# A four-layer transformer kernel: tokens quantised ahead of the weights, bias vectors split side by side in partitions, and six key tiles computed inside the first attention core

## The reference

```python
# layer 0: int8 fake quantisation of normalised tokens and of two weights
s = maximum(max(abs(x), axis=-1) / 127, 1e-8); qdq(x) = clip(round(x / s), -127, 127) * s
q = qdq(layernorm(x)) @ qdq(wq).T + bq
k, v = split(cond @ wkv.T + bkv)
o = softmax(q k^T / 4) v            # 16 heads of 16 features, per sequence
x = x + tanh(g) * (qdq(o) @ qdq(wp).T + bp)
# layer 1, attention: keys of the same context
k1 = cond @ Wkv[:, :256] + bkv[:256]
```

## Time and profile before

| what | value |
|---|---|
| median of 3 runs | 811.41 us (810.72 to 813.89) |
| the profiled execution, its own time | 810.61 us |
| span of the profiled execution, first to last instruction | 808.6 us |
| mean granted clock of PE | 0.978 |
| busy share of the span | PE 88%, DVE 68%, ACT 48%, POOL 45% |
| opening, until the first score matmul of the core | 46.15 us |

### The profile page before, as it was taken

How to read it: one execution, slowest core, us unless ns; L and a number is a source line. 1 busy time by engine, 2 the same in 40 slices (tenths; PEclk the granted TensorE clock), 3 DMA queues, 4 the chain that set the end, 5 groups by cost and what they waited for, 6 DMA issues and landing times.

```text
span 808.6 us, 13964 instructions
## 1 busy us (share of the span) xinstructions
PE 712.4 (88%) x4726; PEld 400.6 (50%) x4726; DVE 552.4 (68%) x1213; ACT 390.0 (48%) x704; POOL 365.1 (45%) x407
## 2 busy tenths in 40 slices
PE   7989899999998877777878898898989999999883
PEld 4644457434553222223335454455469967677431
DVE  5979966467569899999997977865621135126764
ACT  4367724211027998889993554563203343331211
POOL 3523113164413678788885804002240046992335
PEclk9999998899999899999999999999999999999997
DMA  9700003006307899999997004503841141992012
GB/s 309 127 1 1 1 2 98 1 1 131 78 0 143 152 183 196 176 183 193 186 183 110 1 1 122 155 2 114 184 171 61 47 150 59 266 274 59 1 20 33
DMA packets 226764, 84.41 MB, mean 104 GB/s; under 512 B 188755, under 2 KB 224752, under 8 KB 226704
## 3 DMA queue, kind: packets, MB, share of 16 engines
q1 hardware_dynamic: 223760, 78.38, 45.1%
q0 software_dynamic: 2944, 5.25, 2.7%
HBM read 33.26 MB, written 8.40 MB: 52 GB/s over the span
## 4 chain that ended last, share of the span: by engine, by line
PE 48%; DVE 17%; DMA 15%; POOL 10%; issue 6%; ACT 3%; POOLq 0%; DVEq 0%; SPq 0%; ACTq 0%
DMA hT<-hT 8%; POOL hT L1415 5%; PE psum L925 5%; DMA xn<-hT 4%; PE psum L1939 4%; PE psum L896 4%; PE psum L1605 3%; DVE cx L2567 2%; DVE am L808 2%; PE psum L484 2%; POOL moe_in L2070 2%; PE psum L2218 2%; PE psum L638 2%; DVE arena L1732 2%; PE psum L1947 2%
## 5 line engine op out<-in xcount | busy, mean ns | idle before, releaser
L1480 DVE TENSOR_SCALAR_CACHE_REDUCE psum<-psum,arena 128x1024 f32<-128x1024 f32 x128 | 158.6, 1286 | 10.3 <-PE psum L1302 9.5
L355 POOL TENSOR_TENSOR rstd<-ve,neg_half 128x1 f32<-128x1 f32 x64 | 39.6, 623 | 167.3 <-DVE ve L345 166.8
L1302 PE MATMUL psum<-arena 128*128 128x512 bf16 x256 | 79.0, 391 | 37.8 <-ACT arena L1386 24.9
L1415 POOL TENSOR_SCALAR hT<-arena 128x1024 f16<-128x1024 f32 x86 | 89.8, 1044 | 41.6 <-ACT arena L1386 22.2
L1386 ACT ACTIVATE arena<-psum,am 128x1024 f32<-128x1024 f32 x86 | 95.8, 1115 | 15.2 <-POOL hT L1415 9.6
L1302 PEld LDWEIGHTS psum<-arena 128*128 (+1 forms) x256 | 15.2, 97 | 73.3 <-issue 32.9
L1415 POOL TENSOR_SCALAR hT<-sg 128x1024 f16<-128x1024 f32 x42 | 43.9, 1045 | 12.0 <-DMA hT<-hT 4.4
L1386 ACT ACTIVATE sg<-psum,am 128x1024 f32<-128x1024 f32 x42 | 46.8, 1115 | 4.1 <-POOL hT L1415 2.2
L1290 PE MATMUL psum<-hT,arena 128*32 128x256 f16 x352 | 42.6, 282 | 2.2 <-DMA hT<-hT 2.2
L2077 POOL DMA_INDIRECT arena<-moe_out,route x16 | 16.0, 998 | 59.9 <-DMA moe_out<-arena 55.9
L1853 ACT ACTIVATE arena<-psum 128x1024 f32<-128x1024 f32 x32 | 31.0, 1021 | 22.3 <-PE psum L1810 22.3
(11 more groups left out here) (441 smaller groups left out, 1654.0 us busy)
## 6 DMA issues: line engine op xcount, KB each, us to landing
hT<-in_L_ffn_expert_masks SPq DMA_DIRECT2D x32, 256.0 KB, 3.8
arena<-in_L_ffn_w_gate SPq DMA_DIRECT2D x2, 1408.0 KB
arena<-in_L_ffn_w_up SPq DMA_DIRECT2D x2, 1408.0 KB
arena<-in_L_ffn_w_down SPq DMA_DIRECT2D x2, 1408.0 KB
moe_in<-xT SPq DMA_DIRECT2D x2, 1024.0 KB, 6.8
hT<-moe_in SPq DMA_DIRECT2D x4, 512.0 KB, 5.7
moe_out<-arena SPq DMA_DIRECT2D x16, 128.0 KB, 1.7
hT<-hT SPq DMA_TRANSPOSE x83, 3.3
```

Of the source, the lines that this page charges most:

```text
L355: pool.tensor_tensor(rstd[:, t:t + 1], ve[:, t:t + 1], neg_half[:, t:t + 1], ALU.pow).then_inc(sig("ln_rstd"), 1)
L1302: mm = pe.matmul(psum[:, score_banks(c), :][:, g, :], QT[:, bass.ds(row_tile(j, c), 1), pair, :].rearrange("p t q -> p (t q)"), KT[c % 2][ ...
L1415: pool.tensor_scalar(Y1[:, n % Y_SLOTS, :], pe1(n), 255.0, 1024.0, ALU.mult, ALU.add)\
L1480: dve.tensor_scalar(s, s, size1[:, bass.ds(n, 1)], None, ALU.mult, ALU.min, accum_out=am[:, bass.ds(n, 1)])\
```

## The change

- In `xa0_dve` the token tiles are normalised and quantised first, then `w_q0` and `w_p0`. The split of the first bias group stands inside the normalisation, after its fourth round (`BIASES_AT = 3`).
- Biases: there are two groups, of four and of three vectors. Each vector is loaded into 32 partitions of its own (a broadcast of 32 rows instead of 3), so an instruction works on 128 or 96 partitions by 256 elements. A tensor `mask3`, made by one reduction of the identity, picks the three rows in each group of 32. The bias matmul reads three rows at partition 0, 32, 64 or 96. The first group is issued to the SP queue behind the load of `X`, where the two loads stood ahead of it before.
- PE turns the tokens after the values, then `w_q0`, computes the queries, and turns `w_p0` behind them. Both turnings are followed by a wait until ACT has emptied the bank. `xa0_act` has the same order.
- Six key tiles of layer 1 leave the opening. Tile t is computed at step 3 + 4t of the core (t from 0 to 5), at the end of that step, into a bank of `ring_t`; ACT empties it in the step after. `ring_t` and `out0` exchange their banks.

```diff
-        ring_t = Ring([psum[:, i, :] for i in (2, 3)], ...)
+        ring_t = Ring([psum[:, i, :] for i in (0, 1)], ...)
-        FIRST_BIASES = 2
-        bias_parts = sb("bias_parts", [len(BIASES), D], BF16)
+        FIRST_BIASES = 4
+        bias_parts = sb("bias_parts", [2, D], BF16)
+        mask3 = sb("mask3", [3])
+            g, k = divmod(BIASES.index(bias), FIRST_BIASES)
+            rows = slice(32 * k, 32 * k + 3)
+            return pe.matmul(bank[:, 0:D], onesb[rows, :], bias_parts[rows, g, :], start=False, stop=True)
...
+        def biases_dve(dve, step, g):
+            n = min(FIRST_BIASES, len(BIASES) - g * FIRST_BIASES)
+            dve.wait_ge(sig("biases_loaded" if g else "first_biases_loaded"), 16 * n)
+            rows = slice(0, 32 * n)
+            left, parts, flat = bias_left[rows, g, :], [v[rows, g, :] for v in bias_split], bias_parts[rows, g, :]
+            if g == 0:
+                step(dve.tensor_reduce(mask3, identf.rearrange("p (a b) -> p b a", b=32)[:, 0:3, :], AX.X, ALU.add))
...
+        BIASES_AT = 3
+        KEYS1_AT = {3 + 4 * t: t for t in range(6)}
-            return psum[:, b % 2, :]
+            return psum[:, 2 + b % 2, :]
...                                                    # xa0_pe, opening
+            tokens_T_pe(pe, xn, sig("xq_ready"), lambda t: t + 1)
             pe.wait_ge(sig("w0_ready"), DC)
-            weight_T_pe(pe, w_q0)
+            n = weight_T_pe(pe, w_q0)
+            pe.wait_ge(ring_a.evacuated, n)
+            heads(wqT, xT)
             pe.wait_ge(sig("w0_ready"), 2 * DC)
-            weight_T_pe(pe, w_p0)
+            n = weight_T_pe(pe, w_p0)
+            pe.wait_ge(ring_a.evacuated, n)
             pe.wait_ge(sig("kv1_loaded"), 32)
-            keys1_pe(pe, 0, 6)
-            n = tokens_T_pe(pe, xn, sig("xq_ready"), lambda t: t + 1)
-            pe.wait_ge(ring_a.evacuated, n)
-            n = heads(wqT, xT)
-            pe.wait_ge(ring_a.evacuated, n)
...                                                    # xa0_pe, core, behind the value matmuls of a step
+                    if n in KEYS1_AT:
+                        keys1_pe(pe, KEYS1_AT[n], KEYS1_AT[n] + 1, ring_t)
...                                                    # xa0_act, core
+                if n - 1 in KEYS1_AT:
+                    keys1_act(act, KEYS1_AT[n - 1], KEYS1_AT[n - 1] + 1, ring_t)
...                                                    # xa0_dve
-            biases_dve(dve, step, 0, FIRST_BIASES)
+            dve.wait_ge(sig("x_loaded"), 16)
+            norm_dve(dve, 0, lambda t: (sig("x_loaded"), 16), lambda t: biases_dve(dve, step, 0) if t == BIASES_AT else None)
+            qdq_dve(dve, step, [xn[:, t, :] for t in range(NB)], ..., sig("xq_ready"), ...)
             dve.wait_ge(sig("w0_loaded"), 16 * 2)
             for w in (w_q0, w_p0):
                 qdq_dve(...)
-            dve.wait_ge(sig("x_loaded"), 16)
-            norm_dve(dve, 0, lambda t: (sig("x_loaded"), 16))
-            qdq_dve(dve, step, [xn[:, t, :] for t in range(NB)], ...)
             consts_dve(dve, step)
-            biases_dve(dve, step, FIRST_BIASES, len(BIASES))
+            biases_dve(dve, step, 1)
...                                                    # loads0: the first four biases behind X, 32 partitions each
+                    load(sp, bias_left[32 * k:32 * k + 32, g, :], (...).partition_broadcast(32), name)
```

More of the change, by code:

```diff
@@ L467, in biases_dve @@
                     step.wait()
-            step(dve.tensor_scalar(flat, parts[0], identf[0:3, 0:1], None, ALU.mult))
+            step(dve.tensor_scalar(flat, parts[0], mask3[rows, 0:1], None, ALU.mult))
             for i in (1, 2):
                 step.wait()
-                r = dve.scalar_tensor_tensor(flat, parts[i], identf[0:3, i:i + 1], flat, ALU.mult, ALU.add)
+                r = dve.scalar_tensor_tensor(flat, parts[i], mask3[rows, i:i + 1], flat, ALU.mult, ALU.add)
                 if i == 1:
@@ L774, in xa0_dve @@
         def xa0_dve(dve, step):
-            biases_dve(dve, step, 0, FIRST_BIASES)
+            dve.wait_ge(sig("x_loaded"), 16)
+            norm_dve(dve, 0, lambda t: (sig("x_loaded"), 16), lambda t: biases_dve(dve, step, 0) if t == BIASES_AT else None)
+            qdq_dve(dve, step, [xn[:, t, :] for t in range(NB)], [tmp[:, t, :] for t in range(NB)], sig("xq_ready"),
+                    lambda t: dve.wait_ge(sig("ln_ready"), t + 1))
             dve.wait_ge(sig("w0_loaded"), 16 * 2)
@@ L1183, in value_steps1, with keys1_act @@
             dve.reciprocal(inv, size).then_inc(sig("v_steps_ready"), 1)
-        def keys1_act(act, t0, t1):
+        def keys1_act(act, t0, t1, ring=ring_a):
             for t in range(t0, t1):
-                bank = ring_a.take(act)
-                ring_a.release(act.activation(kf[:, t, :], bank[:, 0:D], ACT.Identity, scale=-1.0))
+                bank = ring.take(act)
+                ring.release(act.activation(kf[:, t, :], bank[:, 0:D], ACT.Identity, scale=-1.0))
         def largest1(dve, step, v, scaled, large, size, inv):
@@ L2616, in loads0, with load_biases @@
             load(sp, w_kv0, A["L0_xattn_wkv"].rearrange("(c p) n -> p c n", p=P), "wkv0_loaded")
-            for i, src in enumerate((A["L0_xattn_bkv"][D:2 * D], A["L1_xattn_bkv"][0:D])):
-                load(sp, bias_left[:, i * D:(i + 1) * D], src.partition_broadcast(3), "first_biases_loaded")
             load(sp, X, A["x"].rearrange("b s d -> s b d"), "x_loaded")
+            own = {"L0_xattn_bv": A["L0_xattn_bkv"][D:2 * D], "L1_xattn_bk": A["L1_xattn_bkv"][0:D]}
+            def load_biases(g, name):
+                for k, bias in enumerate(BIASES[g * FIRST_BIASES:(g + 1) * FIRST_BIASES]):
+                    load(sp, bias_left[32 * k:32 * k + 32, g, :], (own[bias] if bias in own else A[bias]).partition_broadcast(32), name)
+            load_biases(0, "first_biases_loaded")
             for dst, name in ((w_q0, "L0_xattn_wq"), (w_p0, "L0_xattn_wp")):
@@ L2625, in loads0 @@
                 load_column(sp, dst, src.rearrange("(c p) -> p c", p=P), "small0_loaded")
-            for i, name in list(enumerate(BIASES))[FIRST_BIASES:]:
-                load(sp, bias_left[:, i * D:(i + 1) * D], A[name].partition_broadcast(3), "biases_loaded")
+            load_biases(1, "biases_loaded")
             loads_ff2(sp)
```

27 lines of the change are left out of this document (9 added, 18 removed).

## The result

The changed kernel took 822.88 us (median of 4 runs, 819.81 to 824.59) beside 812.65 for the kernel before (4 runs, 810.72 to 818.56): ratio 1.011, 95% interval 1.0065 to 1.0156. It is slower by about 1%, clear of noise, and above the forecast's range (808.3 to 815.3). Some executions of every kernel here run longer at a lower granted clock; the ratios compare the faster ones alone, the medians take in all. The profiled execution took 819.81, with a span of 817.8 and a mean granted clock of 0.967.

What follows compares the result with a forecast made beforehand. PE's list bounds the opening; in the core DVE paces, with PE having only 0.48 us spare per period. Opening 5.4 us earlier, core 6.6 longer: net +1.2, so 812.6 us, 8-in-10 range 808.3 to 815.3.

Steps and rivals of the forecast that it cites:

- The core's price: Core: six key tiles ahead of the scores make it 6.6 us longer, bounds 5.7 and 7.6.
- POOL and w_q0: Opening: POOL's kBD0 work beside DVE's quantising of w_q0 adds 0.3 us, bounds 0 and 1.3.
- The rule set beside the sum: Opening: two-port VectorE and GpSimd exclude each other for whole instructions; queries would start up to 2 us later.
- The clock: Opening, rival: the clock falls in PE's lull from 29 to 32, queries 1.5 to 2.3 us longer, 814.5; chance 0.25.
- rival of a slow opening: Opening gains little: core after 43.6, w_q0 ready at 33.6 or later; 815.9 for a core at 44; chance 0.06.
- X: Opening: X, issued 0.76 us earlier, lands at 10.1, bounds 9.7 and 10.45.
- The sum of the opening: Opening: core starts at 40.7 instead of 46.15, 5.4 us earlier, bounds 6.3 and 3.8.
- The bias split's prices: Opening, DVE: first bias split takes about 3.3 us, ending near 16.3, before PE asks at 17.0.
- The second split: DVE: second bias group begins near 32, costs some 3.5 us, ends near 37.
- The bias rows at other partitions: Bias matmuls on PE: taken at no cost; at worst 16 of them would cost about 1 us.
- Behind the core: After the core: PE has 0.48 us a period again, but DVE paces, so nothing is given back.
- low activity: Clock rival's evidence: elsewhere low activity cost the clock, sixteen matmuls taking 9.44 us against 7.10 one round later.

Runs made afterwards that it cites:

- e1: Changed kernel with the six key tiles back in the opening, none in the core, and the old banks; ratio to the kernel before 0.9954.
- e6: Changed kernel with POOL waiting for w_q0, four key tiles in opening pauses, two in the core ahead of the turning; 810.72 us, ratio 0.9927 to the kernel before.
- e10: Changed kernel with each core key tile moved ahead of the turning of the softmax numerators instead of ahead of the scores; core 68.86 us, projection at 116.26.
- e2: Changed kernel with POOL starting its block-diagonal keys only when w_q0 is quantised; ratio to the kernel before 1.0022.
- e5: Changed kernel with the four 32-row bias loads issued behind w_q0 and w_p0; core 70.94 us, projection at 117.38.
- e8: Changed kernel unaltered, profiled again and timed in more rounds; 822.36 us, ratio to the kernel before 1.0054.
- e9: Changed kernel with two of the four 32-row bias loads issued ahead of X and two behind; core 70.91 us, projection at 119.38.
- e3: Changed kernel with 16 unread matmuls of 512 columns between the turned tokens and the wait for w_q0; ratio to the kernel before 1.0075.
- e11: Changed kernel with POOL waiting for w_q0 and unread matmuls, 6 ahead of w_q0's turning and 3 behind it; core from 42.45 us, projection at 113.39.
- e12: Kernel before with X issued ahead of its two 3-row bias loads; core 64.44 us, projection at 110.85.
- e4: Kernel before with only the six key tiles moved into the core and the exchange of banks; ratio to the kernel before 1.0082.

## Why the prediction was wrong

- **The core's price: right.** 6.6 was forecast and 6.5 measured, by the mechanism given: the latency loop through the scores with 0.24 to spare, a period of 7.92. e1 and e6 show that it is the tiles, e10 that it is their place ahead of the scores. Some luck is in the closeness: three tiles and not two cost the whole 1.27, the fourth cost 0.84, and 0.24 came back after the last, where nothing was forecast.
- **POOL and w_q0: the step that failed first.** The prediction took 0.3 us, with 1.3 as the upper bound, for what the two engines do to each other; it was 2.8. The row it used was POOL's own time beside another DVE operation. It priced what POOL lost, and the term needed what DVE would lose. DVE's row of the same stretch stood in the trace before the change, a cast at 1.55 instead of 0.81, and wasn't read. In the changed kernel POOL ran at its own pace and DVE lost all of it. The rule set beside the sum, that of the Trainium skill (SBUF — State Buffer, "Who interferes with whom"), would have given 2 us and was the better guide.
- **The clock: the rival that came true.** It had a chance of 0.25 with a price of 1.5 to 2.3 us; it cost 2.1 on the queries and 0.45 on the turning. Of the profiles with the new order it fell in every one in which the pause stayed unfilled (after, e2, e5, e8, e9, e10), and in none in which matmuls filled it (e1, e3, e6, e11). e3 and e11 differ from their neighbours by the unread matmuls alone, so it is shown. The two weren't independent, as their separate chances made them: w_q0's hold-up made the pause 4.2 us long. The prediction's rival of a slow opening met its condition (core after 43.6, w_q0 after 33.6), but its time, 815.9 for a core at 44, was short too, and it asked for one unknown delay where three stood together.
- **X: mis-sized.** 10.1 was forecast with 10.45 as the upper bound; DVE took it at 11.2 to 12.05 in ten profiles, worth 1.3 us at the last token. The earlier issue gained nothing (e12). The 32-row loads go with 0.7 us or more, where I had put them at nothing because w_q0 isn't wanted early; X was.
- **The sum of the opening.** X costs 1.3, w_q0 costs 2.4 beyond its 2.6, the turning 0.5 (the clock again), the queries 2.1: 6.3, which is the miss (47.05 against 40.7).
- **The bias split's prices: right, its place by luck.** It took 3.2 us (14.26 to 17.48) against 3.3, but ended at 17.5, past the 17.0 at which PE was to ask for it. It held nothing up only because PE's layer-0 keys were late as well in this profile (17.9). In e10, with those keys from 9.85, PE idled 0.59 and began its first value tile at 17.58, just behind the split's end, which then cost nothing further on, since the last token came later. The second split ended at 40.5 and not at 37, by the delays above. e4 confirms that in its old form it would hold DVE to 44.3.
- **The bias rows at other partitions: right at nothing.** The value tiles stand 1.27 us apart as before (19.11 and 20.38), and e1's core equals that before to 0.01 us.
- **Behind the core.** 1.6 us came back in the feed-forward part by the clock, which wasn't foreseen. The sum had nothing there, so of the 7.4 us at the projection 5.8 were left at L896.

## What to carry to other kernels

Work that is moved off an engine's list leaves a pause there, and the pause has a price of its own: look at what the clock does behind it, and put the moved work into such pauses rather than into a stage whose period it lengthens. In a loop of two engines ask for the spare time of each edge, not for busy shares: a tile cost 1.08 ahead of the instruction that the other engine awaits and 0.74 in a place where its own engine idled. When an operation is moved, list what the other engines start on the same event; a pair that was never side by side in the trace has a price that no row gives, and where a similar pair was, read the rows of both engines.

## What the runs showed of the hardware

- DVE's scalings of 256 columns beside POOL's 512-column multiplications took 1.93 for two instead of 0.62, and an operation on 2 columns 0.81 instead of 0.17, while POOL kept its 1.03 each. Beside DVE's 1280-column operations POOL took 1.9 each and a DVE cast 1.55 instead of 0.81, so there both lost. The Trainium skill (SBUF — State Buffer, "Who interferes with whom") describes it as one engine waiting for whole instructions of the other; these rows agree.
- The granted clock fell after a pause as short as 1.5 us with only transposes ahead of it (e2: queries 8.59), and not with 6 matmuls in it and 3 behind the turning (e11: 7.13). A pause of 1.40 us ahead of the token transposes left it at 1.00 (e4: queries 7.13); one of 2.55 us in e4's core was followed by a fall.
- In the kernel before, the clock fell at 137.4 with PE busy 1.00 from 135 to 142, in matmuls of 8 columns (L860). So the slow matmuls of the earlier trace rows follow no idle PE, as the prediction's "low activity" may be read.
- The first turning of w_kv0, eight transposes, took 1.04 to 1.91 us from profile to profile, so that layer 0's keys began anywhere from 9.85 to 11.06. Kernels with the old order show both early and late ones (9.88 and 10.71), and so do those with the new (9.85 and 11.06).
- Issued 0.76 us earlier, the 1 MB load of X landed no earlier (10.45 to 10.75 and 10.6).
